# Window attention and a routed mixture of experts: squares, variances, stores and score bias placed anew

## What is computed

```python
x = x + conv_ref(_ln_c(x), Wq, bq, Wkv, bkv, rel_bias, Wproj, bproj)   # attention in windows of 8 x 8
t = _to_tokens(x)                                                      # (4, 16384, 64)
t = t + ffn_ref(_ln_t(t), router_w, router_b, expert_w, expert_b)
x = _from_tokens(t, x)
...
def _ln_c(v, eps=1e-06):          # over the 64 channels
    m = jnp.mean(v, axis=1, keepdims=True)
    s = jnp.var(v, axis=1, keepdims=True)
    return (v - m) / jnp.sqrt(s + eps)
...
attn = softmax(einsum('bhnd,bhmd->bhnm', q * scale, k) + bias)         # 4 heads of 16, 64 tokens in a window
out = einsum('bhnm,bhmd->bhnd', attn, v) @ Wproj + bproj
...
router_probs = softmax(x @ router_w + router_b)                        # 8 experts
top_p, top_i = top_k(router_probs, 2); top_p = top_p / sum(top_p)
expert_out = einsum('bnd,edc->bnec', x, expert_w) + expert_b
out = einsum('bnk,bnkc->bnc', top_p, gathered(expert_out, top_i))
```

## Time and profile before

| | |
|---|---|
| median of 3 runs | 1271.76 us (1267.67 to 1273.09) |
| the profiled execution | 1272.42 us, of which its span is 1270.6 us |
| granted TensorE clock, mean | 0.973 of full speed |
| TensorE, matmuls busy | 1190.2 us, 94% |
| VectorE busy | 1037.2 us, 82% |
| ScalarE busy | 947.5 us, 75% |
| GpSimd busy | 1081.3 us, 85% |
| chain that ended last, largest shares | TensorE 67%, VectorE 9%, GpSimd 8%, DMA 7%, ScalarE 4% |
| DMA issues, time to landing | x_in 256 KB 3.3 us; t_t 128 KB 2.3 us; out_y 128 KB 2.6 us; recip_rows 16 KB 1.7 us |

### The profile page before, as it was taken

The page is one execution under the profiler, slowest core; times in us unless marked ns, Lnnn a source line. Parts: engine busy times, 40 slices in busy tenths (PEclk is TensorE's granted clock), DMA queues, the critical chain, the costliest instruction groups (busy, mean ns, idle before and its releaser), DMA issues.

```text
span 1270.6 us, 47630 instructions
## 1 busy us (share of the span) xinstructions
PE 1190.2 (94%) x19840; PEld 732.3 (58%) x19840; DVE 1037.2 (82%) x2247; ACT 947.5 (75%) x1743; POOL 1081.3 (85%) x925
## 2 busy tenths in 40 slices
PE   4579999999999999999999999999999999999986
PEld 3356566655556665665565666566566655666531
DVE  3448888888888888888888888889888888888864
ACT  8367888878778888877776888887777777777732
POOL 6267999998888999998888899999988888888753
PEclk8589999999999999999999999999999999999988
DMA  6002333322223233232222323322222222222221
GB/s 184 23 21 70 95 85 82 94 70 54 59 65 83 75 88 102 74 76 62 54 63 62 96 78 91 99 71 63 60 71 54 63 61 70 67 58 63 61 70 42
DMA packets 95623, 91.43 MB, mean 72 GB/s; under 512 B 26929, under 2 KB 62385, under 8 KB 95409
## 3 DMA queue, kind: packets, MB, share of 16 engines
q1 hardware_dynamic: 95408, 88.37, 27.5%
HBM read 35.90 MB, written 17.83 MB: 42 GB/s over the span
## 4 chain that ended last, share of the span: by engine, by line
PE 67%; DVE 9%; POOL 8%; DMA 7%; ACT 4%; issue 4%; DVEq 0%; POOLq 0%; SPq 0%; ACTq 0%
PE bank_y L530 16%; PE bank_s L410 9%; PE bank_t L425 7%; PE bank_s L384 6%; PE bank_o L464 4%; DMA r_b<-recip_rows 4%; PE bank_g L518 3%; PE bank_p L518 3%; PE bank_p L454 3%; PE bank_o L438 3%; DVE prob L880 3%; PE bank_t L362 2%; DMA recip_rows<-r_out 2%; PE bank_t L394 2%; POOL prob L1123 2%
## 5 line engine op out<-in xcount | busy, mean ns | idle before, releaser
L1145 POOL TENSOR_TENSOR t_g<-t_t,g_copy 128x512 f32<-128x512 f32 x192 | 245.8, 1293 | 50.2 <-ACT g_copy L713 49.8
L530 PE MATMUL bank_y<-t_g,w_exp 128*64 128x512 f32 x1024 | 270.2, 620 | 10.1 <-POOL t_g L1145 8.9
L1123 POOL TENSOR_TENSOR prob<-prob,mx 128x512 f32<-128x512 f32 x256 | 261.8, 1044 | 19.2 <-DVE mx L887 19.1
L676 ACT ACTIVATE prob<-prob 128x512 f32<-128x512 f32 x256 | 153.1, 625 | 111.4 <-POOL prob L1123 111.3
L680 ACT ACTIVATE prob_t<-bank_t 128x512 f32<-128x512 f32 x256 | 152.4, 596 | 52.7 <-PE bank_t L425 52.7
L992 DVE TENSOR_TENSOR t_g<-t_t,bank_p 128x512 f32<-128x512 f32 x256 | 174.4, 681 | 17.5 <-PE bank_p L518 12.2
L880 DVE TENSOR_TENSOR prob<-bank_s,rel 128x1024 f32<-128x1024 f32 x128 | 156.3, 1221 | 27.6 <-PE bank_s L410 22.6
L425 PE MATMUL bank_t<-idn,prob 128*128 128x128 f32 x1024 | 163.9, 283 | 7.5 <-ACT v_bd L671 4.0
L410 PEld LDWEIGHTS bank_s<-k_m,q_t 32*64 32x64 f32 x4096 | 113.9, 135 | 91.3 <-issue 58.6
L887 DVE TENSOR_REDUCE mx<-prob 128x16 f32<-128x1024 f32 x128 | 155.4, 1214 | 2.3
L425 PEld LDWEIGHTS bank_t<-idn,prob 128*128 128x128 f32 x1024 | 115.8, 142 | 58.7 <-ACT prob L676 30.7
(11 more groups left out here) (122 smaller groups left out, 2325.3 us busy)
## 6 DMA issues: line engine op xcount, KB each, us to landing
t_t<-t_rout SPq DMA_DIRECT2D x256, 128.0 KB, 2.3
x_in<-in_x SPq DMA_DIRECT2D x68, 256.0 KB, 3.3
r_b<-recip_rows SPq DMA_DIRECT2D x64, 256.0 KB
out_y<-y_out SPq DMA_DIRECT2D x128, 128.0 KB, 2.6
r_in<-sum_b SPq DMA_DIRECT2D x64, 16.0 KB
recip_rows<-r_out SPq DMA_DIRECT2D x64, 16.0 KB, 1.7
t_g<-in_sel SPq DMA_DIRECT2D x1, 512.0 KB, 3.7
rel<-in_relb SPq DMA_DIRECT2D x1, 256.0 KB, 3.0
```

What stands on the lines that cost most here:

```text
L530: mm(B_Y[C * a:C * a + C, :], w_exp[:, pair, :], t_g[:, (2 * pair + a) % TG, :], start=False, stop=(pair == MIXES // 2 - 1), skip_group_ch ...
L676: A(prob[:, i], prob[:, i], ACT.Exp).then_inc(p_ready.sem, 1)
L1123: G.tensor_tensor(sc, sc, mx[:, i, :].unsqueeze(2).broadcast_to([P, 2 * HEADS, NTOK]), ALU.subtract).then_inc(s_shifted.sem, 1)
L1145: G.tensor_tensor(t_g[:, u % TG, :], t_t[:, p, u % 2, :], g_copy[:, n, :], ALU.mult).then_inc(tg_pool.sem, 1)
```

## The change

- `FIRST_SQ` becomes two lists of planes: the squares of the first image are written plane by plane, each plane's 128 pixels side by side, and `first_sums` reads them with the planes as the inner dimensions. The squares of the later images are written as before.
- The variances of the later images move from GpSimd to VectorE, in step PLANES, and the total of the planes moves ahead from step PLANES to step SQUARES. `first_statistics` uses the same function.
- On SP, the stores of a finished strip move from between `cut_sums` and `spread_reciprocals` to behind the latter.
- On VectorE, in slots that take nothing, the bias of the first half of the next strip's scores comes before `normalise` instead of behind it. The maxima stay behind it.
- On GpSimd, in step SCALES, `scale_input` comes behind `gate` 2 instead of before it, as it does in slots with `work.sums`.

```diff
--- before.py
+++ after.py
@@ -152,7 +152,8 @@
         g_copy = sb("g_copy", [P, len(ON_POOL), BANK])
         y_out = sb("y_out", [P, 4, W])
 
-        FIRST_SQ = (x_sq, prob[:, 0:2].rearrange("p i h n k -> p (i h n k)").rearrange("p (h x) -> p h x", x=2 * 4))
+        FIRST_SQ = [flat.rearrange("p (m c h) -> p m c h", m=2, c=4) for flat in (
+            x_sq[:, :, :].rearrange("p h x -> p (h x)"), prob[:, 0:2].rearrange("p i h n k -> p (i h n k)"))]
         B_S = ctx.enter_context(nc.psum_tensor("bank_s", [P, 2, BANK], F32))
         B_T, B_O, B_E, B_P, B_G, B_Y = (
             ctx.enter_context(nc.psum_tensor(f"bank_{n}", [P, BANK], F32)) for n in "toepgy")
@@ -322,10 +323,10 @@
                 projecting, attending, outputting, routing_on, mixing = stages(on)
                 if outputting:
                     cut_sums(j - 1)
+                if outputting:
+                    spread_reciprocals(j - 1)
                 if j > 3:
                     store(j - 4)
-                if outputting:
-                    spread_reciprocals(j - 1)
                 if routing_on:
                     if outputting:
                         sp.wait_ge(recip_spread.sem, recip_spread.at(j - 1, 16))
@@ -619,14 +620,14 @@
                 act.sem_inc(passed, 1)
                 A(dst, src.rearrange("p (c h) -> p c h", c=4), ACT.Copy).then_inc(xt_ready.sem, 1)
 
-            def square_planes(batch, t, r, m, dst=x_sq):
+            def square_planes(batch, t, r, m, first=None):
                 n = batch * GROUPS + t * RING
                 plane = (n % (2 * GROUPS)) * 4
                 act.wait_ge(xt_ready.sem, xt_ready.at(n, 2 * r + m + 1))
                 act.wait_ge(sq_sums.sem, sq_sums.at(batch, max(t * 2 + r - (batch == 0), 0)))
                 act.sem_inc(passed, 1)
-                A(dst[:, :, 4 * m:4 * m + 4].rearrange("p h c -> p c h"), xt[:, bass.ds(plane + (2 * r + m) * 4, 4), :],
-                  ACT.Square).then_inc(sq_ready.sem, 1)
+                dst = x_sq[:, :, 4 * m:4 * m + 4].rearrange("p h c -> p c h") if first is None else first[:, m]
+                A(dst, xt[:, bass.ds(plane + (2 * r + m) * 4, 4), :], ACT.Square).then_inc(sq_ready.sem, 1)
 
             def first_take(batch, t, r):
                 for m in range(2):
@@ -812,16 +813,16 @@
                 V.memset(xc2[:, :, C:C + 1], C * LN_T_EPS).then_inc(set_dve.sem, 1)
                 dve.wait_ge(set_dve.sem, SET_DVE)
 
-            def sum_squares(batch, t, r, src=x_sq):
+            def sum_squares(batch, t, r, src=x_sq[:, :, :]):
                 n = batch * GROUPS + t * RING
                 pair = bass.ds(t * 2 + r, 1)
                 dve.wait_ge(sq_ready.sem, sq_ready.at(n, 2 * r + 2))
                 V.tensor_reduce(sums2[:, :, pair].rearrange("p h o -> p (h o)"),
-                                src[:, :, :], AX.X,
+                                src, AX.X,
                                 ALU.add).then_inc(sq_sums.sem, 1)
 
             def first_sums(batch, t, r):
-                sum_squares(batch, t, r, FIRST_SQ[r])
+                sum_squares(batch, t, r, FIRST_SQ[r].rearrange("p m c h -> p h (m c)"))
 
             def total_squares(batch):
 
@@ -840,10 +841,8 @@
                 V.reciprocal(rstd[:, bass.ds(batch % 2, 1), :].rearrange("p o h -> p (o h)"), st[:, 1, :]
                              ).then_inc(root_turned.sem, 1)
 
-            def first_statistics(batch):
-
-                total_squares(batch)
-                total_planes(batch)
+            def variances(batch):
+
                 dve.wait_ge(totals.sem, totals.at(batch, 2))
                 V.tensor_scalar(st[:, 2, :], st[:, 0, :], 1.0 / C, None, ALU.mult).then_inc(variance.sem, 1)
                 dve.wait_ge(variance.sem, variance.at(batch, 1))
@@ -854,6 +853,12 @@
                 V.tensor_scalar(st[:, 4, :], st[:, 3, :], 0.0, 1.0 / C, ALU.max, ALU.mult).then_inc(variance.sem, 1)
                 dve.wait_ge(variance.sem, variance.at(batch, 4))
                 V.tensor_scalar(st[:, 4, :], st[:, 4, :], LN_C_EPS, None, ALU.add).then_inc(variance.sem, 1)
+
+            def first_statistics(batch):
+
+                total_squares(batch)
+                total_planes(batch)
+                variances(batch)
                 turn_root(batch)
                 r_std = rstd[:, batch % 2, :]
                 half, v = (st[:, n, :] for n in (3, 4))
@@ -1007,8 +1012,9 @@
                     reciprocals(j - 1)
                 if work.step == SQUARES:
                     total_squares(work.batch)
+                    total_planes(work.batch)
                 if work.step == PLANES:
-                    total_planes(work.batch)
+                    variances(work.batch)
                 if work.step == SCALES:
                     turn_root(work.batch)
                 if work.sums:
@@ -1020,10 +1026,13 @@
                     routing(j - 2, 1, 8)
                 if mixing:
                     gate(j - 3, 1 - p, 3)
+                if projecting and not work.take:
+                    bias(j + 1, 0)
                 if outputting:
                     normalise(j - 1)
+                if projecting and work.take:
+                    bias(j + 1, 0)
                 if projecting:
-                    bias(j + 1, 0)
                     maxima(j + 1, 0)
                 if mixing:
                     gate(j - 3, 1 - p, 5)
@@ -1042,19 +1051,6 @@
             G = nc.gpsimd
             G.memset(mhalf[:, :], -0.5).then_inc(set_pool.sem, 1)
             pool.wait_ge(set_pool.sem, 1)
-
-            def variances(batch):
-
-                pool.wait_ge(totals.sem, totals.at(batch, 2))
-                G.tensor_scalar(st[:, 2, :], st[:, 0, :], 1.0 / C, None, ALU.mult).then_inc(variance.sem, 1)
-                pool.wait_ge(variance.sem, variance.at(batch, 1))
-                G.tensor_tensor(st[:, 3, :], st[:, 2, :], st[:, 0, :], ALU.mult).then_inc(variance.sem, 1)
-                pool.wait_ge(variance.sem, variance.at(batch, 2))
-                G.tensor_tensor(st[:, 3, :], st[:, 1, :], st[:, 3, :], ALU.subtract).then_inc(variance.sem, 1)
-                pool.wait_ge(variance.sem, variance.at(batch, 3))
-                G.tensor_scalar(st[:, 4, :], st[:, 3, :], 0.0, 1.0 / C, ALU.max, ALU.mult).then_inc(variance.sem, 1)
-                pool.wait_ge(variance.sem, variance.at(batch, 4))
-                G.tensor_scalar(st[:, 4, :], st[:, 4, :], LN_C_EPS, None, ALU.add).then_inc(variance.sem, 1)
 
             def deviations(batch):
 
@@ -1154,19 +1150,17 @@
                 if attending:
                     shift(j, 2)
                     shift(j, 3)
-                if work.step == PLANES:
-                    variances(work.batch)
                 if work.step == SCALES:
                     deviations(work.batch)
                     scaled_means(work.batch)
                 if work.sums:
                     add_planes(work.batch, *work.sums)
                 normalising = projecting and not (isinstance(j, int) and j == LAST - 1)
-                if normalising and not work.sums:
+                if normalising and not work.sums and work.step != SCALES:
                     scale_input(j + 2)
                 if mixing:
                     gate(j - 3, 1 - p, 2)
-                if normalising and work.sums:
+                if normalising and (work.sums or work.step == SCALES):
                     scale_input(j + 2)
                 if normalising:
                     centre_input(j + 2)
```

## The result

| | before | after |
|---|---|---|
| median | 1271.8 us | 1255.87 us (1255.61 to 1258.25) |
| the profiled execution, its span | 1272.42, 1270.6 us | 1255.74, 1253.9 us |
| VectorE busy | 1037.2 us | 1048.0 us |
| GpSimd busy | 1081.3 us | 1073.4 us |
| write of the reciprocals' row, median | 1.7 us | 1.4 us |

The ratio is 0.9886 with a 95% interval of 0.9864 to 0.9908. The medians differ by 15.9 us and the ratio stands for 14.5, where 20 were forecast. The time lies in the range, 3.9 us above the forecast. All medians are over fast executions; one execution with the old order in SCALES took 1853.94 us at a granted clock of 0.558 and is left out. Which edit gave what came out otherwise than the sum had it.

The account below looks back on a forecast made before the run. TensorE was taken to bound the kernel, so only its idle time counted. The terms 10.1 + 5.1 + 1.5 - 1.2 + 4.5 gave 20.0 us saved: 1252.4 us off the profiled execution, 1251.8 off the median; range 1246 to 1261.

Parts of the forecast that it names:

- Late reciprocals, 10.1 us: Slots outside the take stretches: moving the score bias ahead and the stores behind saves 10.1 us of TensorE's excess, bounds 6 to 10.5.
- the fill: VectorE, non-take slots: the 1.21 us bias fills the wait before normalisation, so a lateness costs only what exceeds 1.54 us.
- Either move alone removes most: Late reciprocals: the bias's move or the stores' move by itself removes most of the 10.1 us, booked once.
- The rival that the stores slow the spread: SP's DMAs: stores in flight with the spread lengthen it by the full 0.9 us, giving 1260 us; chance 0.10.
- PLANES, 5.1 us: Step PLANES: variances moved off GpSimd end TensorE's wait at the experts, 1.7 us in each of three slots, bounds 1.0 to 1.93.
- On VectorE the five cost 1.40: Step PLANES: the five variance instructions take 1.40 us on VectorE, as for the first image, delaying gate 0 by 0 to 0.2.
- SCALES, 1.5 us: Step SCALES: gate 2 ahead of the input's scaling gains 0.5 us in each of three slots, bounds 0 to 1.2.
- The rival on ScalarE: PLANES, SCALES, SQUARES: late exponentials cut gains to 2.9 and 0.9 and SQUARES costs 3.0, giving 1256.4 us; chance 0.12.
- SQUARES, -1.2 us: Step SQUARES: the planes' sum in front of gate 0 costs 0.4 us in each of three slots, bounds 0 to 1.0.
- First image, 3.3 us: First image: plain squares make GpSimd the next bound and start the total of the planes at 29.55, gaining 3.3 us.
- First slots, 1.2 us: First slots, where the pipeline fills and the first group's reciprocals are 5.4 late: the bias ahead gains 1.2 us.
- a write's step costs nothing: First image, ScalarE: squares are slow for another reason and stay so, 3.3 becomes -0.8, giving 1255.9 us; chance 0.03.

## Why the prediction was right, and where it was not

- **Late reciprocals, 10.1 us.** Measured 9.3 in the 34 slots. The size holds, and so does the fill: a lateness of up to 1.5 cost nothing. The step that failed is "Either move alone removes most": the bias alone does, the stores alone take 1 to 4 us. The late write in slot 33 was read as queued behind the stores because they were issued ahead of it. They make about half of the late writes (18 of 34 over 1.9 us in each of the three kernels with them in front, 7 to 11 in the eleven with them behind); the other half, up to 3.3 us, comes with no store in front, and its cause stays open. The rival that the stores slow the spread came only in small, 0.15 us, which the bias covers: 4.3 us of wait are left.
- **PLANES, 5.1 us: the term that failed.** Measured 1.6. The GpSimd side went as told. The step "On VectorE the five cost 1.40 (as they do for the first image" carried a duration from a stretch in which GpSimd was idle to one in which it shifts scores. They cost 2.78, and gate 0, which stands 1.3 us ahead of the copy of the queries when one sum of 1.29 precedes it, stood 0.2 behind it. The lower bound of 1.0 was too high as well: 0.54 a slot came. With the 0.27 lost in SQUARES taken off, the move is worth 0.8 us in all.
- **SCALES, 1.5 us.** Measured 0.9. Right in kind: the later gates stay late. The excess left is 0.98, as in the slot after the last take, so the estimate of 0.75 for 1.2 us of lateness was low. The rival on ScalarE had just this number (0.9); whether the time goes through ScalarE, no run shows.
- **SQUARES, -1.2 us.** Measured -1.6. Twice 0.27, and once 1.07, when the sums of the reciprocals came 0.7 late as well and met a VectorE with nothing to spare.
- **First image, 3.3 us.** Measured 2.8. The squares take 0.63 as forecast and GpSimd binds: its first pair starts at 10.81 and not at 10.6, its pairs take 2.78 instead of 2.71, and the total of the planes starts at 30.11, not 29.55. The sum of squares came to 1.9 us, near its upper bound, and costs nothing.
- **First slots, 1.2 us.** Measured 2.8, at a mean clock of 0.79 instead of 0.76. The bias's move alone gave 0.9 there, at 0.75. The rest had no term in the sum. Over all profiles here these four slots take from 65.1 us at a mean clock of 0.74 to 57.9 at 0.89, so what goes beyond the 0.9 may be the clock, which nothing in the change sets: luck, as far as is known.
- **The rivals.** Two had nearly the measured time and the wrong reason: that a write's step costs nothing (1255.9; the squares went from 1.16 to 0.63) and that ScalarE gives the gains back (1256.4; it was right on the size in SCALES, but in PLANES the held operations came first, and without the root and its tables the slot is 0.11 shorter).

The forecast was 20.0 and the profiled span gave 16.7. PLANES alone is short by 3.5; SCALES 0.6, reciprocals 0.8, first image 0.5 and SQUARES 0.4 make 5.8, and 2.1 came back at the ends and 0.5 in scatter. So the forecast was as near as 3.9 us in part because 2.1 us came that it had no reason for.

## What to carry to other kernels

When work moves to another engine, take its duration from a stretch where the engines around it do what they will do there; one from a quiet stretch is a lower bound. A wait can be covered by placing ready work in front of it, whatever makes it late, and that was worth about three times the removal of the cause that the queue's order suggested (10 us against 3 in the time). Before a cause is read from the order of a queue, look for a late case without it.

## What was not expected of the hardware

- A VectorE operation on SBUF with two sources, or with one and a scalar, that takes 0.23 to 0.29 us alone, ends when GpSimd's instruction does if it is issued while that runs (0.94 to 1.02 us here). A sum of the same size takes 0.29 and one of 1152 elements a partition 1.29 beside the same instruction. One issued within 0.01 us of GpSimd's start was not held, and neither was a reciprocal (0.35). With one of several taken out, the next is held in its place.
- A 16 KB DMA that lands in 1.4 us in most slots took 2.5 in one with the DMA engines' share at 0.08 and no store ahead of it, and up to 3.3 in others.
- PLANES slots are now and then 1.5 to 2.8 us longer with a mean granted clock of 0.92. Before each such spell TensorE had waited 1.7 to 2.0 us. In the kernel with the store's move alone that spell begins at TensorE's wait for the experts:

```profile
301.58 1.80 PE L530 MATMUL bank_y<-t_g,w_exp 128*64 128x512 f32 x4 [1.75 <-POOL t_g L1145]
```

The four matmuls took 1.80 instead of 1.08. The kernel before has the same wait and no such spell in the profiled execution, and the wait of 1.95 without the bias's move had none either, so the wait does not decide it alone.
